# Gate logits from x1 by a premade product, and a head, a preparation and a block end spread over other steps, in a GRU and mixture-of-experts kernel

## What is computed

```python
# layer 0: a GRU over 512 time steps, h0 = cond_2048, then a base product and low-rank experts
r = sigmoid(i_r + h_r); z = sigmoid(i_z + h_z); n = tanh(i_n + r * h_n)
h = (1 - z) * n + z * h                         # one step; gi = x @ W_ih + b_ih, gh = h @ W_hh + b_hh
top 2 of softmax(h @ router_w.T)                # weights of the 8 experts of rank 16
x1 = x + h @ weight.T + sum_e w_e * 2 * (h @ A_e.T) @ B_e.T
# layer 1: resample x1 along the features at 512 grid points per batch (linear), then top 2 of 8 experts
x2 = w0 * x1[..., i0] + w1 * x1[..., i1]        # the same as x1 @ gm, gm a 512x512 matrix per batch
logits = x2 @ gate_w.T + gate_b
out = x1 + sum over the top 2 of weight * ((glu * sigmoid(1.702 glu) * (lin + 1)) @ w2_e.T + b2_e)
```

## Time and profile before

| | before |
|---|---|
| median of 3 runs without profiler | 2033.37 us |
| profiled execution (its span) | 2053.76 us (2051.9 us) |
| TensorE busy, products | 1696.2 us, 83% |
| VectorE busy | 1410.8 us, 69% |
| ScalarE busy | 750.2 us, 37% |
| GpSimd busy | 285.6 us, 14% |

### The profile page before, as it was taken

How to read it: one execution, slowest core, us unless ns; L and a number is a source line. 1 busy time by engine, 2 the same in 40 slices (tenths; PEclk the granted TensorE clock), 3 DMA queues, 4 the chain that set the end, 5 groups by cost and what they waited for, 6 DMA issues and landing times. The chain is left out here.

```text
span 2051.9 us, 90285 instructions
## 1 busy us (share of the span) xinstructions
PE 1696.2 (83%) x38301; PEld 1095.2 (53%) x38301; DVE 1410.8 (69%) x6376; ACT 750.2 (37%) x2706; POOL 285.6 (14%) x581
## 2 busy tenths in 40 slices
PE   6777767778679999968599999978699999776995
PEld 4565555555445556545456566545456555442442
DVE  6888888887757777767677777767677777641221
ACT  5544444442323343322233343323233333322332
POOL 0111111121121111120211011120211111201001
PEclk9999999999989999999899999989899999987997
DMA  8444343422055464422265555240545464228995
GB/s 311 174 145 157 129 157 141 157 95 85 22 204 193 172 248 176 144 64 64 85 213 185 210 214 178 82 116 3 186 183 193 172 213 152 69 60 304 348 356 164
DMA packets 113621, 334.86 MB, mean 163 GB/s; under 512 B 41920, under 2 KB 42168, under 8 KB 100800
## 3 DMA queue, kind: packets, MB, share of 16 engines
q1 hardware_dynamic: 108096, 312.31, 42.8%
q0 software_dynamic: 5120, 16.78, 2.5%
HBM read 263.74 MB, written 65.32 MB: 160 GB/s over the span
## 5 line engine op out<-in xcount | busy, mean ns | idle before, releaser
L480 PE MATMUL bank_g<-whh,hs_early 128*32 128x256 f16 x8192 | 324.6, 279 | 257.7 <-DVE hs_early L972 247.9
L1261 POOL COPY hxs<-hs 128x32 f16<-128x32 f16 x512 | 221.7, 433 | 1519.6 <-DVE hs L977 1519.6
L727 ACT ACTIVATE rz<-pre 128x32 f32<-128x32 f32 x512 | 118.9, 232 | 804.2 <-DVE pre L960 804.2
L480 PEld LDWEIGHTS bank_g<-whh,hs_early 128*32 128x32 f16 x8192 | 173.8, 97 | 435.0 <-DVE hs_early L972 424.0
L958 DVE STREAM_TRANSPOSE xt<-bank_g 128x256 f32<-128x256 f32 x512 | 229.7, 449 | 201.8 <-PE bank_g L486 196.4
L626 PE MATMUL bank<-wm,wih 128*128 128x512 f16 x1440 | 351.1, 384 | 2.8 <-issue 1.6
L493 PE MATMUL bank_g<-whh,hs 128*32 128x128 f16 x16384 | 331.4, 222 | 6.6 <-issue 6.1
L486 PE MATMUL bank_g<-whh,hs 128*32 128x256 f16 x8192 | 321.6, 278 | 1.4 <-issue 1.1
L493 PEld LDWEIGHTS bank_g<-whh,hs 128*32 128x32 f16 x16384 | 290.5, 99 | 14.0 <-issue 10.3
L727 ACT ACTIVATE seq_h<-na 128x16 f32<-128x16 f32 x512 | 111.6, 218 | 283.2 <-DVE na L966 283.2
L486 PEld LDWEIGHTS bank_g<-whh,hs 128*32 128x32 f16 x8192 | 191.1, 98 | 43.5 <-DVE hs L977 3.3
(11 more groups left out here) (139 smaller groups left out, 1863.4 us busy)
## 6 DMA issues: line engine op xcount, KB each, us to landing
wm<-moe_split SPq DMA_DIRECT2D x60, 1536.0 KB
wm<-moe_split SPq DMA_DIRECT2D x60, 1024.0 KB
wm<-moe_split SPq DMA_DIRECT2D x60, 512.0 KB
wm<-in_w_moe SPq DMA_DIRECT2D x16, 1536.0 KB, 10.9
moe_split<-wm SPq DMA_DIRECT2D x16, 1536.0 KB, 6.4
wih<-x_rows SPq DMA_DIRECT2D x60, 256.0 KB, 7.6
y_rows<-wih SPq DMA_DIRECT2D x60, 256.0 KB, 4.9
xr<-in_x SPq DMA_DIRECT2D x16, 512.0 KB, 7.0
```

The lines of the kernel that those rows point to most:

```text
L480: mm(bank_g[0][32 * j:32 * j + 32, 0:2 * P], early_cols[:, 4 * B * k:4 * B * k + 32], whh[:, 1, k, at:at + 2 * P], start=(k == 0), stop=False)
L727: return nc.scalar.activation(dst, src, func, **kw)
L1261: Q.tensor_copy(hxs[:, par, :, :, :, col].rearrange("p s k b -> p s (k b)"), hs_new).then_inc(S["h_kept"], 1)
```

## The change

- **Gate logits**: in block 0, TensorE transposes gm (`turn_grid`, 128 transposes), ScalarE copies them (`grid_out`), and TensorE multiplies them by the gate weights (`gate_grid`, 192 products of 8 columns); the product, split once, is `gws`. In the head the logits come from x1's halves by `gws`, in steps 15 and 16. `turn_x2` and its copies are gone; VectorE makes the low halves of x2 from the bank, as before, and only the scatter reads them.
- **Head**: 29 steps in place of 30. `lora`, x1, its split and the copies go by 512 columns, one a step, in 7 to 10, 7 to 10, 11 to 14 and 8 to 11; the base products spread to step 9; samples in 12 to 20, the first two batches interleaved by k; routing in 16 to 18; rank, tile counts and slots all in 19; `eid` in 20; splits of x2 in 18, 20, 21, 22. Scatter behind `keep` of 20 to 23, its wait for x2 per batch.
- **End**: 9 steps (`TAIL`); the last 13 down products all in its first; gather behind `keep` of 121 to 124; scaling, combining and the last transposes and adds in the same steps 123 to 127 as before.
- **Preparation**: x of visit 1, b2, identity and constants move into block 0 (steps 0, 1, 106 and 107, 116 to 118); the products of visit 1 start at step 2, in 14 steps; ScalarE runs one sigmoid at its start (`warm`).
- **Block 0**: VectorE's subtraction and absolute value become one `Abs` of ScalarE with a bias; the grid operations, x and its loads stand in other steps, no two of VectorE's added pieces in one step.

The core of the diff:

```diff
-HEAD = 30
+HEAD = 29
+TAIL = 9
-BASE_CUT = {2: (0, 8), 3: (8, 16), 4: (16, 24), 6: (24, 32), 7: (32, 40), 8: (40, 48)}
-SAMPLE_CUT = {11: (0, 6), 12: (6, 14), 13: (14, 22), 14: (22, 30), 15: (30, 39), 16: (39, 48)}
+SAMPLE = [(b, k, w, a) for k in range(K) for b in (0, 1) for w, a in PARTS] + \
+         [(b, k, w, a) for b in (2, 3) for k in range(K) for w, a in PARTS]
+BASE_CUT = {2: (0, 8), 3: (8, 16), 4: (16, 24), 5: (24, 26), 6: (26, 34), 7: (34, 38), 8: (38, 43), 9: (43, 48)}
+SAMPLE_CUT = {12: (0, 6), 13: (6, 12), 14: (12, 18), 15: (18, 19), 16: (19, 20), 17: (20, 27), 18: (27, 34),
+              19: (34, 41), 20: (41, 48)}
+GRID_START = (4, 26, 48, 70)
+GRID_DVE = {s + at: (b, j) for b, s in enumerate(GRID_START) for j, at in enumerate((0, 1, 4, 8, 12, 16))}
+GRID_ABS = {s + 2 + 4 * k: (b, k) for b, s in enumerate(GRID_START) for k in range(K)}
+X_LO = [s + q for s in (13, 21, 35, 53, 67, 89) for q in range(2)]
+X_LOAD = {15: 3, 24: 4, 38: 5, 56: 6, 70: 7}
+TURN_AT = {s: (b, j) for b, at in enumerate(((67, 68, 69, 70), (74, 75, 78, 79), (86, 87, 90, 91), (95, 96, 98, 99)))
+           for j, s in enumerate(at)}
+GW_AT = {s + k: (b, k) for b, s in enumerate((71, 80, 92, 100)) for k in range(K)}
+GW_HI, B2_AT, B1_AT, CONST_AT = 104, 106, 110, 116
...
             def gate(f, b):
-                pe.wait_ge(S["x2t_out"], f * B + b + 1)
+                if b == 0:
+                    pe.wait_ge(S["x1_lo"], (f + 1) * K)
                 for j, (k, w, a) in enumerate(LOW):
-                    i = mm(p_log[:, b], xgt[b % 2][:, a, k], wgs[:, w, k], start=(j == 0), stop=(j == len(LOW) - 1))
+                    i = mm(p_log[:, b], x1s[:, a, k, b], gws[:, w, b, k], start=(j == 0), stop=(j == len(LOW) - 1))
...
+            def gate_grid(b, k):
+                pe.wait_ge(S["gmt_out"], (b + 1) * K)
+                pe.wait_ge(S["l0_split"], 4)
+                for n, (j, w, a) in enumerate(LOW):
+                    i = mm(p_gw[:, b, k], gmt[j][:, a, k], wgs[:, w, j], start=(n == 0), stop=(n == len(LOW) - 1))
...
             def last_down(f, i):
-                if i < 2:
-                    down(f, NT // 2, 0, 3 + i)
-                if i >= 4:
-                    b = i - 4
+                if i == 0:
+                    down(f, NT // 2, 0, 3)
+                    down(f, NT // 2, 0, 4)
+                if i >= 5:
+                    b = i - 5
...
+            def grid_abs(b, k):
+                act.wait_ge(S["grid_chain"], b * GRID_CHAIN + 2)
+                run(g_a, g_t, ACT.Abs, scale=-1.0, bias=iotf[:, k:k + 1]).then_inc(S["grid_a"], 1)
...
+            act.wait_ge(S["warm"], 1)
+            run(warm, warm, ACT.Sigmoid)
...
-            x_lo(1, 0)
-            x_lo(1, 1)
-            dve.wait_ge(S["b2_hi"], 1)
-            stt_(b2_split[:, 1], b2f, WS, b2_split[:, 0], ALU.mult, ALU.subtract).then_inc(S["row_split"], 1)
-            dve.wait_ge(S["const_in"], 16 * 3)
-            step(V.memset(ones_f[:, :], 1.0))
...
             def scatter(f, b):
                 if b == 0:
                     pool.wait_ge(S["slots_done"], f + 1)
-                    pool.wait_ge(S["x2_lo"], (f + 1) * B)
                     pool.wait_ge(S["xt_mm"], f * NT) if f else pool.wait_ge(S["zeroed"], 16 * NT)
+                pool.wait_ge(S["x2_lo"], f * B + b + 1)
...
-                steps(0, 23)
+                steps(0, 20)
                 for b in range(B):
-                    steps(23 + b, 24 + b)
+                    steps(20 + b, 21 + b)
                     scatter(f, b)
```

More of the change, by code:

```diff
@@ L359, in _ @@
                 v, at, n = visit(s)
+                if s in X_LOAD:
+                    load_x(X_LOAD[s])
                 if v is not None:
-                    if at == 4 and v + 2 < NB:
-                        load_x(v + 2)
                     if v not in KEPT and at == n // 2:
@@ L784, in grid_hi, with grid_out @@
                 run(gm[:, 0, b, k], g_r, ACT.Copy).then_inc(S["grid_hi"], 1)
+            def grid_out(b, j):
+                act.wait_ge(S["gmt_mm"], b * K + j + 1)
+                if b:
+                    act.wait_ge(S["gw_mm"], b * K)
+                run(gmt[j], half_l[0], ACT.Copy).then_inc(S["gmt_out"], 1)
             def l0_hi(q):
@@ L900, in blk @@
                         slot(f, j // 2, j % 2, u, more=j + 1 < NT)
-                for i in range(FT - HEAD - NT * SLOT):
+                for i in range(TAIL):
                     step(HEAD + NT * SLOT + i)
@@ L1037, in prelude @@
                 moe_lo(s)
[L1038 to L1041 removed]
+                if s in X_LO:
+                    x_lo(v + 1, X_LO.index(s) % 2)
+                if s == 1:
+                    x_lo(1, 0)
+                    x_lo(1, 1)
+                if s == B2_AT + 1:
+                    dve.wait_ge(S["b2_hi"], 1)
+                    stt_(b2_split[:, 1], b2f, WS, b2_split[:, 0], ALU.mult, ALU.subtract).then_inc(S["row_split"], 1)
+                if s == CONST_AT:
+                    step(V.memset(ones_f[:, :], 1.0))
+                    V.memset(ones[:, :], 1.0)
+                    V.memset(ones_as[:, :], AS)
+                if s == CONST_AT + 1:
+                    dve.wait_ge(S["const_in"], 16 * 3)
+                    step(V.tensor_tensor_scan(tri[:, :], ones_f[:, :], idt[:, :], 0.0, ALU.mult, ALU.add))
+                    step(tt_(tri[:, :], tri[:, :], idt[:, :], ALU.subtract))
+                if s == CONST_AT + 2:
+                    step(V.tensor_copy(iott[:, 0:E], iote[:, :]))
+                    step(ts_(iott[:, E:], iote[:, :], float(E), None, ALU.add))
+                    step(ts_(full[:, :], iote[:, 0:K], float(P), None, ALU.mult))
+                if s in GRID_DVE:
+                    grid_op(*GRID_DVE[s])
+                if s == GW_HI + 1:
+                    dve.wait_ge(S["gw_hi"], 1)
+                    stt_(gws[:, 1], p_gw, 1 / WS, gws[:, 0], ALU.mult, ALU.subtract).then_inc(S["gw_split"], 1)
                 if s in L0_LO:
                     l0_lo(*divmod(L0_LO.index(s), 2))
[L1044 removed]
+                if s == B1_AT + 2:
                     dve.wait_ge(S["b1_hi"], 1)
```

285 lines of the change are left out of this document (133 added, 152 removed).

## The result

The changed kernel takes **1979.87 us** in the median of four runs (1975.15 to 1985.12), beside 2037.17 us (2032.92 to 2041.77) for the kernel before: a ratio of 0.972, 95% interval 0.968 to 0.976. Faster was right. The profiled execution took 1976.15 us, with a span of 1974.3.

What follows compares the result with a forecast made beforehand. Bound taken: a chain of 3.20 us per GRU step through TensorE, VectorE and ScalarE, 1638 of 2051.9 us. Five parts (-4.2, -5.4, -14.4, -2, -8.5) sum to -34.5, from median 2033.4 to 1999 us; range 1987 to 2021.

Steps and rivals of the forecast that it cites:

- Part 4: Scatter and gather, blocks 1 to 3: earlier gather -4.7, against it +2.4 and +1, rows some tenths: -2 us, range -8 to +6.
- (a): Rival: frozen steps of scatter and gather cost 2 to 3 us more in six places, +15, so 2014 us; chance 0.22.
- Part 3: Head in blocks 1 to 3: excess over the step floor falls from 6.7 to 1.9 us per block, together -14.4 us.
- Part 2: The 128 steps of block 0: VectorE operations removed, -7.2, against added work: -5.4 us, range -8 to -2.
- Part 1: Preparation: VectorE's work ahead of the first step moves into later steps, so the first L958 starts 4.2 us earlier.
- Part 5: Last block: logits and slots ready earlier, scatter starts 8.8 us earlier: -8.5 us, range -10 to -5.
- (b): Rival: a DMA pair straddling L958 freezes L958 and L962, doubling the price in six places, +60, so 2059 us; chance 0.05.
- (c): Rival: ScalarE's Abs causes 32 table loads, +36 us, so 2035, no change; chance 0.07 with other losses of that size.
- (d): Rival: last block's gate products stay behind all samples, its gain only -3, so 2004 us; counted in the forecast's 0.63.

Runs made afterwards that it cites:

- e6: The kernel before, unaltered, run again beside the unaltered changed kernel: 2038.13 us.
- e17_lead: Changed kernel with GpSimd waiting for both gate groups ahead of each DMA pair, scatter pairs two steps later, gather pairs one: 2018.95 us, ratio 0.991.
- e4_shift: The kernel before with 128 more instructions (waits already met) at the start of TensorE's program: 2068.78 us, ratio 1.005.
- e3_early: The kernel before with each indirect DMA pair of blocks 1 and 2 moved ahead of GpSimd's copy (keep) of its step: 2048.00 us, one run.
- e12_after_third: The changed kernel, unaltered, run again: 2026.48 us, one run.
- e15_after_fourth: The changed kernel, unaltered, run again beside the kernel before: 2027.07 us, ratio 0.987.

## Why the prediction was right or wrong

- **The step that failed** is one sentence of the sum: that the profiled run was 1% above the median, but "the parts are stretches of engine work that run alike in both". They do not. The profile of before was held, the timed runs free. Between the spans of the two (2051.9, and 2036.0 in e6) lie 15.9 us, and the excess of the scatter's steps alone differs by 15.0. For a profiled run, held, the forecast was 2019, with the parts' bounds 2008 to 2034; measured there were 2026.48 and 2027.07, 27 to 30 us below before in place of 34.5. Free, another 27 us come from the places of part 4, priced at 2.
- **Part 4**, scatter and gather: "worth at most a few tenths" for the rows, and "-4.7" for ScalarE's waits, with 2.4 and 1 against them. The price was read from steps in which the freeze already covered the wait. Held, the two places changed by +0.3 us together, near the -2. Free, by -27.3, and `e17_lead` gives 30 of it back. The range had room for -8. The wait row, 26.5 us in 15 waits, was the right one, but of it "the half and less" was taken because "the frozen chain is the next limit there": true only of the held profile. Two readings of the earlier trace rows fell short besides. L962 did not wait for the work of TensorE's last third: its products end at 1005.95, 2.5 us ahead of L962, and only the signal was late. And L962's wait of 2.20 is not longer than the pair, as rival (a) has it: the pair takes 2.31.
- **Part 3**, heads: mechanism right, size not. Steps 1 to 19 came as worked out (step 19 4.01 against 4.05, 20 3.67 against 3.7, most of the rest 3.20 to 3.32), and steps 0 to 20 of block 3 keep an excess of 2.1 us, against 1.9. The term is too small, 14.4 against 17.0 to 20.6, because the 6.7 of block 3 stood for all three blocks; blocks 1 and 2 had 7.9 and 8.9 in the same profile.
- **Part 2**, block 0: -0.1 and +1.4 against -5.4. Missing was that TensorE stalls where a page comes late. Block 0 of the changed kernel takes 431.1 to 439.6 over the four places of the page ends that were tried, and that of the kernel before 433.3 (`e4_shift`) to 437.7 over two; that 431.1 is near the 432 foretold is luck of the place. The work's part was too large as well. If each step of block 0 is given the shortest length that any trace of its kernel shows (before: five traces, two places of the page ends; after: fifteen, four places), the sums are 430.1 and 426.8. By this estimate the work is worth 3.3 us and not 5.4. A piece of what is missing is step 64, for which the sum has no term. The Trainium skill (Runtime: NRT & Kernel Launch, "Instruction fetch mechanics") has the same 256 instructions in a block of 16 KiB and calls the cost of crossing mostly hidden; the trace agrees on the size and not on the cost, with gaps of up to 2.75 us and 8 us between the shortest and the longest block 0.
- **Part 1**: -4.06 in the profile, -5 in the pairs of traces, against -4.2. **Part 5**: -9.1 and -10.7 against -8.5 (from trace to trace of the changed kernel's variants the last block differs by up to 7); the scatter starts 11.0 earlier instead of 8.8.
- **Rivals.** (a), dearer freezes, +15: held, the places cost what they had cost; it fell. (b), a pair astride L958 doubles the price: fell by `e3_early`, and by `e12_after_third` and `e15_after_fourth`, whose first pair does stand astride the end of step 20 and whose scatter costs what it cost before. (c), table loads by Abs, fell: one load is left. The Trainium skill (ScalarE: Activation LUTs, "Table sets: the hidden batching unit") has abs in every set; the trace agrees for the one set that is loaded here. (d) fell: the logits are read 12.0 us earlier against the last step. By the rule of the Trainium skill on the shared port (SBUF - State Buffer, "SBUF: two separate sides") the splits of steps 20 to 22 could hold up the pairs. The trace of the changed kernel can't tell: no split overlaps a pair by more than 0.16 us, and the pairs' DMAs last 0.96 to 1.03 beside them, as without (1.16 for the first of block 1).

## What to carry to other kernels

When a profiled run lies 1% above the timed ones, find the row that makes the difference before pricing anything by it: here one wait with releaser "remote" gave the condition away, and the frozen steps covered the waits that the timed runs really had. A transfer wants its lead counted in steps from the last instruction that triggers it to the first that uses it, and a wait read behind another stall is a lower bound of its worth. If indirect DMAs stand in a latency-bound loop, start them just behind the last signal that the loop waits for: it cost 6 us where it was not needed and saved 37 where it was.

## What the runs showed of the hardware

- In the held condition the signals of TensorE reach VectorE mostly 0.45 to 0.7 us after the end of a pair of indirect DMAs of 2.3 us (not always: in `e12_after_third` L990 starts at 989.58, 0.18 ahead of the end of the pair, and in `e15_after_fourth` at 985.65, between its two DMAs), though its products are done, and products that fall into a pair can come in pieces (0.20 to 0.50 us apart in `e3_early`); in the free condition the same pair at the same 0.08 us behind L958 delays nothing (0.75 against 2.94 us from L958 to L962). VectorE's sum L960 and ScalarE's sigmoid beside the pair take 0.25 and 0.23 us in both. By which path GpSimd's DMAs hold TensorE, and what decides between the conditions, stays open; dropping a pair or its second DMA was not tried.
- TensorE's program comes in packets of 16 KB. In block 0 of the changed kernel 62 of 74 followed the one before by 3.3 to 7.5 us and the other 12 by 7.7 to 10.9, and where the products were dense TensorE ran dry for up to 2.75 us. Why these packets start late stays open too.
- Waits of TensorE that are already met are not free: 128 instructions with two such waits each (`e4_shift`) moved the first step from 37.1 to 50.6 us, 0.1 us for each instruction.
- GpSimd's copy of the state takes 0.64 us in the mean in block 0 of the changed kernel, where VectorE splits weights beside it in every step, and 0.37 in block 2.
